# Linear attention of layer 1: W_out folded into the masked sums of keys and values, queries scaled by the inverse denominators

## The reference, cut to what matters

```python
q_feat = jax.nn.elu(q * SCALE) + 1.0
k_feat = jax.nn.elu(k) + 1.0
kv = jnp.einsum('bhtd,bhtv->bhdv', k_feat, v)
k_sum = k_feat.sum(axis=2)
denom = jnp.maximum(jnp.einsum('bhtd,bhd->bht', q_feat, k_sum), 1e-06)
out = jnp.einsum('bhtd,bhdv->bhtv', q_feat, kv) / denom[..., None]
out = out.transpose(0, 2, 1, 3).reshape(B, T, D)
return out @ W_out
```

## Time and profile before

| | |
|---|---|
| median of 3 runs | 980.91 us (980.83 to 981.66) |
| the profiled execution's own time | 979.83 us |
| its span | 978.2 us |
| PE matmul busy | 865.8 us (89%) |
| PE weight load busy | 773.9 us (79%) |
| DVE busy | 674.3 us (69%) |
| ACT busy | 515.4 us (53%) |
| POOL busy | 181.2 us (19%) |

### The profile page before, as it was taken

The page is one execution under the profiler, slowest core; times in us unless marked ns, Lnnn a source line. Parts: engine busy times, 40 slices in busy tenths (PEclk is TensorE's granted clock), DMA queues, the critical chain, the costliest instruction groups (busy, mean ns, idle before and its releaser), DMA issues. The chain is left out here.

```text
span 978.2 us, 16165 instructions
## 1 busy us (share of the span) xinstructions
PE 865.8 (89%) x5619; PEld 773.9 (79%) x5619; DVE 674.3 (69%) x1287; ACT 515.4 (53%) x907; POOL 181.2 (19%) x198
## 2 busy tenths in 40 slices
PE   3898202799799999999999999999979999999998
PEld 3687101799699999899999989999878787978877
DVE  7786000454666878878787787888477979889764
ACT  3632000433555564664756465475438867678581
POOL 1004775000000000000000000000612526153202
PEclk9999555899999999999999999999989999999999
DMA  8772446000544766666567665653300203021101
GB/s 263 265 253 76 151 156 218 1 1 2 163 131 150 230 229 214 214 220 209 190 207 244 216 211 203 221 197 103 92 23 22 65 19 98 16 76 53 43 1 44
DMA packets 93871, 134.24 MB, mean 137 GB/s; under 512 B 8608, under 2 KB 78688, under 8 KB 93824
## 3 DMA queue, kind: packets, MB, share of 16 engines
q1 hardware_dynamic: 85024, 107.80, 33.6%
q0 software_dynamic: 8800, 25.83, 7.9%
HBM read 98.22 MB, written 35.39 MB: 137 GB/s over the span
## 5 line engine op out<-in xcount | busy, mean ns | idle before, releaser
L1061 PE MATMUL ps<-w2h,hh 128*128 128x256 f32 x568 | 162.8, 287 | 0.0
L1063 PE MATMUL ps<-w2h,hl 128*128 128x256 f32 x568 | 160.7, 283 | 0.0
L1062 PE MATMUL ps<-w2l,hh 128*128 128x256 f32 x568 | 160.7, 283 | 0.0
L1201 ACT ACTIVATE h<-ps,b1T 128x512 f32<-128x512 f32 (+1 forms) x160 | 90.5, 588 | 132.7 <-PE ps L1063 132.5
L1306 DVE TENSOR_TENSOR hl<-h,hh 128x512 fp32r<-128x512 f32 x124 | 85.5, 689 | 66.1 <-ACT hh L1205 65.2
L1061 PE MATMUL ps<-xTh,w1h 128*128 128x512 f32 (+1 forms) x320 | 110.7, 346 | 2.4 <-DVE xTl L1248 2.4
L1050 POOL DMA_DIRECT2D expert_out<-y x28 | 20.5, 733 | 492.3 <-DVE y L1265 492.3
L1062 PE MATMUL ps<-xTl,w1h 128*128 128x512 f32 (+1 forms) x320 | 110.6, 346 | 0.0
L1061 PEld LDWEIGHTS ps<-w2h,hh 128*128 128x128 f32 x568 | 108.7, 191 | 2.4 <-DVE hl L1306 0.2
L1062 PEld LDWEIGHTS ps<-w2l,hh 128*128 128x128 f32 x568 | 108.8, 192 | 2.1
L1063 PE MATMUL ps<-xTh,w1l 128*128 128x512 f32 (+1 forms) x320 | 109.9, 343 | 0.0
(11 more groups left out here) (306 smaller groups left out, 2262.9 us busy)
## 6 DMA issues: line engine op xcount, KB each, us to landing
raw<-in_L_ffn_W SPq DMA_DIRECT2D x30, 1024.0 KB
raw_odd<-in_L_ffn_W SPq DMA_DIRECT2D x28, 1024.0 KB, 6.8
dispatched<-shared SPq DMA_DIRECT2D x1, 9088.0 KB, 32.1
expert_out<-y POOLq DMA_DIRECT2D x11, 512.0 KB, 3.6
rows<-dispatched SPq DMA_DIRECT2D x20, 256.0 KB, 3.4
shared<-in_L_ffn_b SPq DMA_DIRECT2D x9, 512.0 KB, 8.3
xn_rows<-raw SPq DMA_DIRECT2D x4, 1024.0 KB, 5.2
rows<-xn_rows SPq DMA_DIRECT2D x32, 128.0 KB
```

What stands on the lines that cost most here:

```text
L1061: pe.matmul(out, ah, bh, start=start, stop=False, skip_group_check=True)
L1062: pe.matmul(out, ah, bl, start=False, stop=False, skip_group_check=True)
L1063: return pe.matmul(out, al, bh, start=False, stop=stop, skip_group_check=True)
L1201: op = act.activation(h32[:, at, cols], ps[:, slot, cols], ACT.Relu, bias=s.b1T[:, ds(e * HC + w * tile.chunks + n, 1)])
```

## The change

The weighted sum and the output projection are both linear, so W_out can be multiplied into the masked sums once per sequence, and the division moved to the queries. Per body, now:

- `turn_sums`: 2 transposes of the masked sums (bank 4); ACT copies them to `kvT`.
- `fold_out`: 2 products kvT x wout, 256 columns (bank 5); ACT copies them to `folded_out`.
- `denominators`: 16 products qT x key sums of 8 columns (bank 2), for all 8 tiles and both c.
- `invert` on DVE: one clip and one reciprocal, 128x128.
- ACT spreads each inverse over its head's 16 features, two activations of 128x1024.
- `spread_quotients(h)`: 8 transposes of the spread inverses per half.
- `scale_queries(h)` on DVE: qT times the turned inverses, two operations of 128x512 per half.
- `project_out(h)`: scaled qT times `folded_out`, as many matmuls as before.

`quotients`, `divide`, `turn_attention` and the copies to `oT` are gone. The small new tiles are cut out of one tile `beyond_gate`, and stand under this name in the lists of instructions.

```diff
-                def quotients(pairs):
-                    for n in pairs:
-                        if n >= 2:
-                            pe.wait_ge(gated, NG * b + 2 * (n - 1))
-                        for i in (2 * n, 2 * n + 1):
-                            for c in range(DC):
-                                mm = pe.matmul(ps[:, (2 + i) % 8, c * (P + HP):(c + 1) * (P + HP)],
-                                               qT[:, c, tile_of(i)], kv[:, c, :], start=True, stop=True)
-                        mm.then_inc(nd_mm, 1)
...
+                def fold_out():
+
+                    pe.wait_ge(fold_ready, 2 * b + 1)
+                    for c in range(DC):
+                        mm = pe.matmul(ps[:, 5, c * D:(c + 1) * D], kvT[:, c, :], wout[:, c, :], start=True, stop=True)
+                    mm.then_inc(fold_mm, 1)
+
+                def denominators():
+
+                    pe.wait_ge(qT_ready, 4 * b + 4)
+                    for i in range(BT):
+                        for c in range(DC):
+                            mm = pe.matmul(ps[:, 2, (DC * i + c) * HP:(DC * i + c + 1) * HP], qT[:, c, tile_of(i)],
+                                           sums[:, c, :], start=True, stop=True)
+                    mm.then_inc(den_mm, 1)
...
-                mix_values(range(3))
-                pe.wait_ge(qT_ready, 4 * b + 4)
-                pe.wait_ge(kv_ready, b + 1)
-                quotients([0, 1])
+                mix_values([0])
+                turn_sums()
+                mix_values([1])
+                fold_out()
+                denominators()
+                mix_values([2])
+                spread_quotients(0)
                 mix_values([3])
-                quotients([2])
-                turn_attention(0)
-                quotients([3])
+                spread_quotients(1)
                 project_out(0)
-                turn_attention(1)
                 if not last:
+                    pe.wait_ge(gated, NG * b + NG)
                     turn(b + 1, 0)
                 project_out(1)
```

On ACT:

```diff
                 if not last:
-                    for u in range(2):
-                        deviation(b + 1, u)
-                        normalized(b + 1, u)
-                for m in range(4):
-                    h, c = m // 2, m % 2
-                    act.wait_ge(att_turned, 4 * b + m + 1)
-                    act.activation(oT[:, c, h * HB:(h + 1) * HB], ps[:, 2 + c, :], ACT.Copy).then_inc(oT_ready, 1)
+                    deviation(b + 1, 0)
+                act.wait_ge(fold_mm, 4 * b + 1)
+                act.activation(kvT[:, :, :], ps[:, 4, 0:DC * P].rearrange("p (c f) -> p c f", c=DC), ACT.Copy
+                               ).then_inc(fold_ready, 1)
...
+                act.wait_ge(den_step, 2 * b + 2)
+                for h in range(2):
+                    act.activation(
+                        spread_inverse[:, 4 * h:4 * h + 4].rearrange("p i c (h f) -> p (i c h) f", f=HD),
+                        inverse[:, 4 * h:4 * h + 4].rearrange("p i c h -> p (i c h)").unsqueeze(2).to_broadcast(
+                            [P, 4 * DC * HP, HD]), ACT.Copy).then_inc(spread, 1)
+                if not last:
+                    normalized(b + 1, 0)
+                    deviation(b + 1, 1)
+                    normalized(b + 1, 1)
```

More of the change, by code:

```diff
@@ L1372, in combine_and_layer1, with words @@
         act_k, gate = sb("act_k", [P, DC, T]), sb("gate", [P, BT, D])
-        oT, att = sb("oT", [P, DC, T]), sb("att", [P, BT, D])
+        beyond_gate = sb("beyond_gate", [P, 4 * T])
+        space = iter(range(4 * T // P))
+        def words(n):
+            first = next(space)
+            for _ in range(n // P - 1):
+                next(space)
+            return beyond_gate[:, first * P:first * P + n]
+        den, inverse = (words(P).rearrange("p (i c h) -> p i c h", i=BT, c=DC) for _ in range(2))
+        spread_inverse = words(BT * D).rearrange("p (i c f) -> p i c f", i=BT, c=DC)
+        folded_out = words(DC * D).rearrange("p (c e) -> p c e", c=DC)
+        kvT = words(DC * P).rearrange("p (c f) -> p c f", c=DC)
+        sums = words(P)[:, 0:DC * HP].rearrange("p (c h) -> p c h", c=DC)
         prob = qk[:, :, :, :].rearrange("p u j e -> p u (j e)")
@@ L1404, in combine_and_layer1 @@
             "qT_mm", "qT_ready", "kv_mm", "kv_ready", "v_mm", "gated"))
-        nd_mm, den_clipped, den_inv, att_ready, att_turned, oT_ready = (sem(n) for n in (
-            "nd_mm", "den_clipped", "den_inv", "att_ready", "att_turned", "oT_ready"))
+        den_mm, den_step, spread, q_scaled, fold_mm, fold_ready = (sem(n) for n in (
+            "den_mm", "den_step", "spread", "q_scaled", "fold_mm", "fold_ready"))
         wh_ready, wl_ready, xh_ready, xl_ready = (sem(n) for n in ("wh_ready1", "wl_ready1", "xh_ready1", "xl_ready1"))
@@ L1742, in turn_attention, with turn_sums @@
[L1742 to L1746, removed]
+                def turn_sums():
+                    pe.wait_ge(kv_ready, b + 1)
+                    for c in range(DC):
+                        mm = pe.transpose(ps[:, 4, c * P:(c + 1) * P], kv[:, c, :], s.ident[:, :])
+                    mm.then_inc(fold_mm, 1)
[3 more added lines that the diff above has]
+                        mm = pe.matmul(ps[:, 5, c * D:(c + 1) * D], kvT[:, c, :], wout[:, c, :], start=True, stop=True)
+                    mm.then_inc(fold_mm, 1)
@@ new lines, in denominators, with spread_quotients @@
+                def denominators():
+                    pe.wait_ge(qT_ready, 4 * b + 4)
+                    for i in range(BT):
+                        for c in range(DC):
+                            mm = pe.matmul(ps[:, 2, (DC * i + c) * HP:(DC * i + c + 1) * HP], qT[:, c, tile_of(i)],
+                                           sums[:, c, :], start=True, stop=True)
+                    mm.then_inc(den_mm, 1)
+                def spread_quotients(h):
+                    pe.wait_ge(spread, 2 * b + h + 1)
+                    if h == 0:
+                        pe.wait_ge(fold_ready, 2 * b + 2)
@@ L1747, in turn_attention @@
                     for c in range(DC):
                         for i in range(4):
-                            mm = pe.transpose(ps[:, 2 + c, tile_of(i)], att[:, 4 * h + i, tile_of(c)], s.ident[:, :])
-                        mm.then_inc(att_turned, 1)
+                            mm = pe.transpose(ps[:, 4 - 2 * h + c, tile_of(i)], spread_inverse[:, 4 * h + i, c, :],
+                                              s.ident[:, :])
+                    mm.then_inc(fold_mm, 1)
                 def project_out(h):
-                    pe.wait_ge(oT_ready, 4 * b + 2 * (h + 1))
+                    pe.wait_ge(q_scaled, 2 * b + h + 1)
@@ L1872, in body @@
                 if not first:
-                    act.wait_ge(nd_mm, NG * b)
+                    act.wait_ge(out_mm, NG * b)
                 scaled(b)
@@ L2098, in apply_gate, with invert, scale_queries @@
                     V.tensor_tensor(at, pair_of_tiles(ps[:, (6 + n) % 8, :]), at, ALU.mult).then_inc(gated, 1)
[L2100 to L2112, removed]
+                def invert():
+                    dve.wait_ge(den_mm, b + 1)
+                    V.tensor_scalar(den[:, :, :, :], ps[:, 2, 0:P].rearrange("p (i c h) -> p i c h", i=BT, c=DC), 1e-6, None,
+                                    ALU.max).then_inc(den_step, 1)
+                    dve.wait_ge(den_step, 2 * b + 1)
+                    V.reciprocal(inverse[:, :, :, :], den[:, :, :, :]).then_inc(den_step, 1)
+                def scale_queries(h):
+                    dve.wait_ge(fold_mm, 4 * b + h + 3)
+                    at = slice(h * HB, (h + 1) * HB)
+                    for c in range(DC):
+                        op = V.tensor_tensor(qT[:, c, at], ps[:, 4 - 2 * h + c, :], qT[:, c, at], ALU.mult)
+                    op.then_inc(q_scaled, 1)
                 if not last:
@@ L2126, in body @@
                     measure(b + 1, 1)
+                invert()
                 apply_gate(0)
@@ L2130, in body @@
                     scales(b + 1, 1)
-                divide(0)
-                divide(1)
+                scale_queries(0)
                 apply_gate(2)
                 apply_gate(3)
-                divide(2)
-                divide(3)
+                scale_queries(1)
                 for n in range(NG):
```

16 lines of the change are left out of this document (10 added, 6 removed).

## The result

| | before | after |
|---|---|---|
| median of the runs, us | 980.87 (979.96 to 981.66, 4 runs) | 993.43 (991.70 to 995.19, 4 runs) |
| ratio, 95% interval | | 1.0128 (1.0114 to 1.0142) |
| profiled execution, us | 979.83, span 978.2 | 991.7, span 990.1 |

The change makes the kernel 12.6 us slower. The forecast was 991.4 us in a range of 986.5 to 997.0, with 0.92 on slower. The median lies in the range, 2 us above the forecast.

A forecast was written before the change was run, and what follows sets the result against it. PE's list was taken to bound layer 1. Three sequences 3.2 us longer and the last 0.9 made 10.5 us, added to the median of 980.91 for 991.4 us, in a range of 986.5 to 997.0.

The forecast's parts named there:

- What bounds layer 1: In layer 1 the time is the length of PE's list; work inserted there, or waits, count in full.
- The denominators: On PE, 16 products per sequence as 32 matmuls, 0.112 us each by the pace of loads, 3.57 us.
- naked loads: Rival for the denominators on PE: weight loads not overlapped, 0.19 us each, 1001.4 us in all; chance 0.06.
- the first rival: Narrow denominator products on PE are really cheap, down to 0.2 us in all: 978.8 us, not slower; chance 0.07.
- First wait: PE waits 0.95 us for ACT's spreads of the inverses, before their transposes, in all four sequences.
- Second wait: PE waits 1.4 us for DVE's scaled queries ahead of project_out(0), in three sequences, not in the last.
- Sum: Layer 1 longer by 3.2 us in three sequences and about 0.9 in the last, 10.5 us in all.
- the clock: Rival: PE's granted clock falls around the denominators, 12.9 us more at most, middle 998 us; chance 0.07.
- PEclk 1.00 throughout: Sign expected in the profile: PE's granted clock stays full, with no fall.
- the forecast's own range: 988.5 to 994.5 us, for reciprocal and spread 0.3 us a sequence either way, loads between 0.107 and 0.117.

The follow-up runs named there:

- den64: The changed kernel with each denominator product streaming 64 columns instead of 8: 909.04 us, 1.0110 of the kernel before; a repeat gave 909.10 us, 1.0099.
- inter: The changed kernel with the denominator products spread, four after each wide product of the second pair's values, ahead of the fold: 910.99 us, 1.0130 of the kernel before.
- den1: The changed kernel with only one of the 16 denominator products issued, results wrong, for timing alone: 897.28 us, 0.9973 of the kernel before.
- actorder: The changed kernel with the next normalization and second square root ahead of the spreads in ACT's list: 908.93 us, 1.0084 of the kernel before.
- order64: The changed kernel with 64-column denominator products, these ahead of the fold, and scale_queries(0) ahead of scales(b + 1, 1): 902.79 us, 1.0029 of the kernel before.
- again: The changed kernel run once more unedited, on another chip: 912.56 us, 1.0143 of the kernel before.
- again2: The changed kernel unedited a further time, beside a 64-column kernel on the same chip: 910.60 us, 1.0120 of the kernel before.

## Why the prediction was right, and where it was off

- **What bounds layer 1** (PE's list): right. The stage became 2.97 longer in each undisturbed sequence with a successor and the layer's end moved with it.
- **The denominators**, 3.57 us by the pace of loads: measured 3.49. The choice was between 0.2 by columns and 6.1 by naked loads. den64 shows that columns have next to no part in it, inter that wide neighbours hide nothing, den1 that without this product nothing is lost. The rule of the Trainium skill ("TensorE: Matmul & The Clock Gate", section "LDWEIGHTS (loading the stationary operand)", 107 ns for 128 columns) agrees with the measured 109. The gap of about 25 ns in the Trainium skill, same page, section "Back-to-back issue gap", which stood with the first rival, is not approached by these 109 ns; here every matmul brings its load.
- **First wait**, for ACT's spreads, forecast 0.95: shown as 0.63, and 0.87 by the starts (8.03 + 1.73 to 10.63). The reciprocal took 0.95 instead of 0.97, and the two spreads 2.00 together instead of 2.2 (the prediction has them end at 11.87 and then goes on from 11.74; measured, ACT went on at 11.43).
- **Second wait**, for the scaled queries behind the next normalization, forecast 1.4 in three sequences and none in the last: shown as 1.01, with PE's list free at 14.17 and `project_out(0)` at 15.34. It is in the sequences where the clock held. actorder removes it by ACT's list, order64 by DVE's and an earlier block of denominators.
- **Sum**: 3 x 3.2 + 0.9 = 10.5 forecast, 3 x 2.97 + 0.83 = 9.7 measured at full clock; den64, whose clock holds at the stage, cost 9.3 and 8.2 in time.
- **The step that was mis-sized** is the clock. It stood as a rival of 0.07, beside the forecast "PEclk 1.00 throughout". It is no alternative to the sum but an addition to it, and in the three profiled executions of the unedited change (after, again, again2) it comes in 5 of 12 sequences. Its price was set as "12.9 at most; much of a short fall hides in the waits", and the second half of that is what came: no fall cost more than 2.5 us. With 1.2 us for it in the profiled execution the sum is 10.9, and with the 1.1 from layer 0 the 11.9 seen there is told. The median is 0.7 above that execution's difference; whether the others had more falls stays open, since they have no trace. So does the reason for a fall: that it goes with the undivided 8-column block is shown, why it comes in one sequence and not in the next is not.
- 993.4 lies even in the forecast's own range of 988.5 to 994.5, but that range was drawn for the reciprocal, the spreads and the loads, and these came out 0.8 us below the forecast. The 2.8 us on top of them lay outside its terms: in the profiled execution the fall and the later start in layer 0, in the others unknown. That two errors of opposite sign left only 2 us is luck; the mechanism of the other 9.7 is not.

## What to carry to other kernels

A product whose moving side shrinks below what its weight load takes gets no cheaper: 136 columns became 8, the time per matmul went from 0.116 to 0.109 us, and what had come along with the quotients' stationary tile had to be computed elsewhere. Where the moving side is this narrow, count loads, not columns, and ask which format needs only one. And where a new result passes through three engines, look in each list at what stands ahead of its step: here two exchanged steps were worth 6.3 us of a loss of 8.2.

## What the runs showed of the hardware

- A block of 32 matmuls of 8 columns, 3.5 us at 1.00 PE busy in the trace, went with a granted clock of 0.50 in it or within 1.3 us behind it in 12 of 20 cases; the same block with 64 columns, also 3.5 us and 1.00 busy, never did, in 20. den1, with two such matmuls, showed no fall at the stage either. Spread over 5.2 us the block had none in four sequences of one execution, but three others without a trace had mean clocks of 0.983 to 0.985.
- A matmul of 32-bit floats with a new stationary tile takes 0.109 us at 8 and 0.110 at 64 columns; in the reduced format a product needs one in place of two, 1.89 / 16 = 0.118 us each.
- A reciprocal of 128x128 elements on DVE took 953 ns, against 353 for 128x32.
